# Preparing the first scan unit inside the routing program, and spreading the scatters over two units

## The reference

```
hidden [8,512,256]
layer 0, mixer : a two-directional state space layer (512 channels, 16 states):
                 xn = layernorm(x); xz = W_in xn; per direction: 4-tap convolution, silu,
                 x_dbl = Wx x -> dt (64), B (16), C (16); dt = softplus(Wdt dt + b)
                 for each state n: h[t] = exp(dt*A[n]) * h[t-1] + dt*B[n]*x ; y += C[n]*h
                 y = (y_forward + y_backward + x*D) * silu(z); s = W_out y
layer 0, experts: scores = Wr xn (8 experts), the best 2 of each token, weighted;
                 each expert: silu(a)*b of a 256->1024 product, then 512->256
layer 1        : linear attention with a memory (16 heads, chunks of 128), a three-level MLP
                 (256->1024->256) and a gate from W x + C V^T x
```

## Time and profile before

| | us |
|---|---|
| median of 3 runs (3166.04 to 3168.67) | 3166.66 |
| the profiled execution | 3172.15 |
| its span, first to last instruction | 3170.4 |
| TensorE / VectorE / ScalarE / GpSimd busy | 2612.1 / 2253.1 / 1776.4 / 1738.3 |
| granted TensorE clock, mean | 0.922 |

### The profile page before, as it was taken

One profiled execution on the slowest core, in us unless ns is written; L12 is line 12 of the kernel. 1 busy time (PEld: TensorE's weight loads), 2 busy tenths in 40 slices (PEclk: granted clock), 3 DMA queues, 4 the chain that ended last, 5 costly groups with the idle time before them and its releaser, 6 DMA issues. The chain is left out here.

```text
span 3170.4 us, 40091 instructions
## 1 busy us (share of the span) xinstructions
PE 2612.1 (82%) x13342; PEld 1723.8 (54%) x13342; DVE 2253.1 (71%) x2790; ACT 1776.4 (56%) x2731; POOL 1738.3 (55%) x550
## 2 busy tenths in 40 slices
PE   5357788787787887878878878657999999999999
PEld 5134565565565565565555555545556455555554
DVE  5399999989989989989989989984343442442430
ACT  1367777767867958858858858522332332332322
POOL 0598879869878878878778788851000000000000
PEclk9777899899999989989989989767999999999999
DMA  6223333333334333324333333213000000000000
GB/s 254 84 77 120 111 110 116 133 117 118 111 115 141 115 107 122 131 88 145 112 103 126 136 107 118 70 53 116 26 33 0 33 33 0 33 33 0 7 7 7
DMA packets 144229, 274.85 MB, mean 87 GB/s; under 512 B 23095, under 2 KB 94238, under 8 KB 143006
## 3 DMA queue, kind: packets, MB, share of 16 engines
q1 hardware_dynamic: 137886, 255.70, 23.7%
q0 software_dynamic: 6144, 16.79, 1.6%
HBM read 231.80 MB, written 40.63 MB: 86 GB/s over the span
## 5 line engine op out<-in xcount | busy, mean ns | idle before, releaser
L745 POOL TENSOR_TENSOR hs<-u,bb 128x2048 f32<-128x2048 f32 x256 | 1159.0, 4536 | 288.4 <-PE hT L1087 249.0
L947 DVE TENSOR_TENSOR_SCAN hs<-dA,hs 128x1024 f32<-128x1024 f32 x512 | 1163.1, 2278 | 96.5 <-POOL hs L745 72.6
L1087 PE MATMUL hT<-ident,hs 128*128 128x128 f32 x3616 | 586.3, 304 | 362.2 <-DVE held L957 312.1
L842 ACT ACTIVATE dA<-dt,cols 128x511 f32<-128x511 f32 x1024 | 661.4, 680 | 318.0 <-DVE hs L947 313.0
L1087 PEld LDWEIGHTS hT<-ident,hs 128*128 128x128 f32 x3616 | 443.5, 154 | 521.8 <-DVE held L957 370.5
L957 DVE SCALAR_TENSOR_TENSOR held<-hT,ct,held 128x512 f32<-128x512 f32 x872 | 604.5, 733 | 22.7 <-PE hT L1087 22.1
L1361 ACT ACTIVATE gl<-bank,cols_sb 128x512 f32<-128x512 f32 x192 | 130.7, 687 | 527.1 <-PE bank L1600 526.8
L1600 PE MATMUL bank<-mT,cms_sb 128*128 128x512 f32 x768 | 362.6, 597 | 10.1 <-ACT mT L1355 8.6
L138 POOL COPY cur<-slot 128x8 uint32 (+1 forms) x8 | 1.5, 190 | 626.7 <-DVE held L150 626.2
L1106 PEld LDWEIGHTS moe<-xgT,held 128*128 128x128 f32 x2272 | 289.0, 205 | 54.3 <-issue 26.4
L1106 PE MATMUL moe<-xgT,held 128*128 128x128 f32 x2272 | 302.9, 290 | 13.0 <-ACT xgT L857 13.0
(11 more groups left out here) (232 smaller groups left out, 3295.6 us busy)
## 6 DMA issues: line engine op xcount, KB each, us to landing
held<-wl SPq DMA_DIRECT2D x71, 1024.0 KB
bb<-b_scratch SPq DMA_DIRECT2D x128, 512.0 KB
held<-wl SPq DMA_DIRECT2D x71, 512.0 KB
xg<-xg_scratch SPq DMA_DIRECT2D x71, 128.0 KB
yg_scratch<-yg SPq DMA_DIRECT2D x71, 128.0 KB, 1.7
held<-x SPq DMA_DIRECT2D x16, 512.0 KB, 8.6
xg_scratch<-zero SPq DMA_DIRECT2D x8, 1024.0 KB, 4.7
cb<-b_scratch SPq DMA_DIRECT2D x30, 256.0 KB, 4.4
```

What stands on the lines that cost most here:

```text
L745: nc.gpsimd.tensor_tensor(hs[n % HS][:, :, :], u[d][:, :, :], row, ALU.mult).then_inc(dBu_ready, 1)
L842: last = nc.scalar.activation(dst, src, ACT.Exp, scale=cols[:, at:at + 1])
L947: nc.vector.tensor_tensor_scan(h, decay, h, 0.0, ALU.mult, ALU.add).then_inc(scan_done, 1)
L1087: last = nc.tensor.transpose(hT[c % 2][:, k * P:(k + 1) * P], hs[n % HS][:, k, c * P:(c + 1) * P], ident[:, :])
```

## The change

- **The first unit's preparation moves into the routing program.** Its products stand between the turns and scores of the batches on TensorE, its copies between the roots and copies on ScalarE; the weights are loaded between the batches of `x`. The eight products that build the convolution's `taps` move from VectorE to GpSimd; `xpad`'s second copies from VectorE to ScalarE. Batch 0 is turned straight into `xnT`, which is no longer stored and loaded. `soft` of the first unit is the end of VectorE's routing program. B's rows are stored and the first two pairs loaded there too.
- **Scores turned round**: `w_r`, widened to 32 columns, is stationary and `xaT` moves (two products of 512 columns a batch, four batches in one bank), then four transposes a half. Choice and weights are worked out in two halves of 16 chunks.
- VectorE takes the variance of batch b+1 before it normalises batch b, and ScalarE's roots stand one batch ahead.
- **Scatters over two units**: none before the first state; 8 chunks (`EARLY`, now 8) in states 0 to 2 of unit 0, one chunk in each of its other 13 states, 11 in unit 1. VectorE waits for the first eight before its first weighing, no longer before the unit loop.
- **Tiles**: unit 1 has one (at slot 25), units 2 to 15 five each. The first tiles are loaded at state 11 of unit 1.

```diff
-        EARLY = 18
+        EARLY = 8
+        OPEN = 3
+        GROUPED = 11
...
-                    last = scores(b)
+                def scores(b):
                     pe.wait_ge(aT_ready, KD * (b + 1))
+                    g, h = b % QB, b // QB
+                    for k in range(KD):
+                        last = nc.tensor.matmul(bankR[4 + h][RG * g:RG * (g + 1), :], w_r[:, k, :], xT(b)[:, k, :],
+                                                start=(k == 0), stop=(k == KD - 1))
...
+                turn_rows(0); turn_rows(1); scores(0); piece("proj", 0)      # TensorE, one line each in the code
+                turn_rows(2); scores(1); piece("proj", 1); turn_rows(3); scores(2)
+                piece("conv", 0); piece("proj", 2); turn_rows(4); scores(3); piece("conv", 1); piece("proj", 3)
+                turn_rows(5); turn_scores(0); scores(4); piece("conv", 2); turn_rows(6); scores(5)
+                piece("conv", 3); turn_rows(7); scores(6); scores(7); turn_scores(1)
+                piece("xd", 0); piece("dt", 0); piece("dt", 1)
+                pe.wait_ge(chosen, 2)      # the two counting products, then c, dt 2, dt 3
...
+                choose(0)                  # VectorE
+                choose(1)
+                weights(0)
                 dve.wait_ge(cnt_ps, 1)     # rows and owners as before
...
+                weights(1)
+                dve.wait_ge(setup_a, 1)
+                nc.vector.tensor_scalar(a_cols, a_cols, -1.0, None, ALU.mult)
+                for quarter in range(4):
+                    soft(dve, 0, 0, quarter)
...
-                for c in range(TC - EARLY, TC):
-                    group(c, grouped[0])
+                def groups(unit, n):
+                    if unit_is_first(unit):
+                        return range(TC - EARLY, TC)[3 * n:3 * n + 3] if n < OPEN else (n - OPEN,)
+                    return (NS - OPEN + n,) if unit_is_first(unit - 1) and NS - OPEN + n < TC - EARLY else ()
...
-                            if not later(unit) and n < TC - EARLY:
-                                group(n, grouped[1])
+                            for c in groups(unit, n):
+                                group(c, grouped[int(c < TC - EARLY)])
...
-                for i in range(-T0, 0) if d == 0 else range(NT - TPB * (NB - 1) if last else TPB - T0):
+                for i in range(1) if first else range(FIRST_TILE[d], FIRST_TILE[d] + TPU):
```

More of the change, by code:

```diff
@@ L20 @@
 HP = P // 2
+QB = NB // 2
+RG = P // QB
+QC = NC * QB
 EPS = 1e-5
@@ new lines, in plan @@
+        def plan(d, what, at):
+            for k, s in enumerate(at):
+                PREP[d][s].append((what, k))
+        plan(0, "proj", (0, 1, 4, 7))
+        plan(0, "conv", (3, 6, 8, 10))
+        plan(0, "silu", (10,))
+        plan(0, "xd", (12,))
+        plan(0, "dt", (14, 16, 18, 20))
+        plan(0, "soft", (21,))
+        plan(0, "c", (16,))
+        plan(1, "gate", (20, 21, 22, 24))
+        plan(1, "conv", (4, 6, 7, 8))
+        plan(1, "silu", (8,))
+        plan(1, "xd", (10,))
@@ new lines, in bass_mamba_moe_then_linear_attention_mlp @@
+        plan(1, "dt", (11, 12, 13, 15))
+        plan(1, "soft", (16,))
+        plan(1, "c", (17,))
+        OUT = {0: 0, 2: 1}
+        SKIP = (0, 2, 3, 4)
+        SOFT = ((13, 14, 15, 15), (15, 15, 15, 15))
+        LATE = ((3, 6, 15, 19, 21, 23, 28), (3, 5, 6, 16, 17, 18, 19, 20, 21, 22, 25, 28, 30))
+        FIN = (0, 0, 1, 1)
+        WEIGH, ADD = ((1, 2), (2, 2)), ((3, 3), (3, 3))
+        USES = [[use for s in range(2 * NS) for use in PREP[d][s] if use[0] not in ("silu", "soft")] for d in range(2)]
@@ L329, in tt, with variance @@
                     ch.link(nc.vector.tensor_tensor(o, a, c, op))
-                for b in range(NB):
+                def variance(b):
                     cs = range(NC * b, NC * (b + 1))
@@ L341, in _ @@
                     nc.vector.tensor_scalar(rs[:, cs[0]:cs[-1] + 1], mv[:, cs[0]:cs[-1] + 1, 1], EPS, None, ALU.add).then_inc(var0, 1)
+                variance(0)
+                for b in range(NB):
+                    cs = range(NC * b, NC * (b + 1))
+                    if b + 1 < NB:
+                        variance(b + 1)
                     dve.wait_ge(std0, b + 1)
@@ L359, in _ @@
[L359 to L370, removed]
+                def over(row, whole):
+                    return row.rearrange("p (c e) -> p c e", c=1).broadcast_to(whole)
@@ L408, in _ @@
[L408 to L412, removed]
+                weights(1)
+                dve.wait_ge(setup_a, 1)
+                a_cols = cols[:, AL:AL + 2 * DB * NS]
@@ L585, in units @@
                 for d in range(2):
-                    yield d, 2 * b + d, tile_pieces(d, last) if d == 1 or later(b) else NONE, not (last and d == 1)
+                    yield d, 2 * b + d, tile_pieces(d, not later(b)) if d == 1 or later(b) else NONE, not (last and d == 1)
             def batches(eng, body):
@@ L593, in batches @@
                 body(NB - 1, True)
-            def unit_is_first(unit):
-                return not later(unit)
             block = lay0.enter_context(nc.Block())
```

630 lines of the change are left out of this document (353 added, 277 removed).

## The result

The changed kernel takes 3161.41 us (median of 20 runs, 3155.33 to 3167.34) against 3166.87 us of the kernel before on the same chip (20 runs): ratio 0.9981, interval 0.9974 to 0.9988. So it is 0.2% faster there. On another chip, where the kernel before takes 3154.66 us, the same two kernels gave 1.0022 (1.0013 to 1.0031), 0.2% slower. The second comparison came with the experiments, and it is the more instructive one.

A forecast was written before the change was run, and what follows sets the result against it. It saw TensorE, then VectorE, leading the routing, an engine-to-engine preparation chain, and GpSimd and VectorE in units 0 and 1. Terms -57.2 + 29.4 + 3.1 + 15.8 = -8.9 us gave a median of 3158, range 3144 to 3173.

The forecast's parts named there:

- First state at 90.3, -57.2: Routing and preparation: unit 0's first state starts near 90.3 us instead of 147.54, -57.2 us, bounds -63 and -50.
- TensorE's 48.3 us of work: Routing: TensorE's turns, scores, projections, convolutions and score transposes until the second half's scores are turned, summed to 48.3 us.
- The GpSimd `taps`: Routing: eight operations, some 10 us on GpSimd, needed only near 30 us; no cost was added for them.
- The score product, bounds 1.0 and 3.58: Routing on TensorE: a batch's two products of 512 columns taken at a projection's 1.92 us; 3.58 was the old form.
- the three "remote" waits: Old preparation: ScalarE waits of 3.63, 8.06 and 3.67 us that no engine or transfer explains.
- The first rival: Routing: the 15.4 us of unexplained ScalarE waits move along with the preparation, giving 3173 us; chance 0.12.
- Scatters, +17.8 and +11.6: Units 0 and 1: scatters between states add 17.8 us in unit 0 and 11.6 in unit 1, +29.4 in all.
- the rival with 27.5: Unit 1: GpSimd's idle time doesn't take the scatters, costing up to 27.5 us instead of 11.6; chance 0.18.
- Last unit +3.1: Last unit: four more tiles, three of whose gates on VectorE fall before the last scan, +3.1 us, bounds 0 and 4.
- Tail +15.8: Tail: the gather waits for the store of the last tile's `down`, now at slot 30; +15.8 us, bounds 12 and 20.
- Everything behind shifts whole: After the tail's gather: the norm, the output and the barrier behind it shift whole, by the tail's +15.8 us.
- The rule weighed: Routing: crossing instruction blocks is mostly hidden and a taken branch stalls, so the long straight program costs nothing; time 3158.

The follow-up runs named there:

- e_taps: The changed kernel with the eight taps made by VectorE behind its normalisation of the third batch, not by GpSimd: 3161.88 us, ratio 1.0021 to the kernel before.
- e_oldscores: The changed kernel with the scores' products as before, 8 columns each and nothing turned: 3183.54 us, ratio 1.0089 to the kernel before.
- e_noscatter: The changed kernel with the 64 scatters and the waits for them left out: 3122.70 us, ratio 0.9897 to the kernel before.
- e_tail: The changed kernel with the last unit's five tiles five slots apart, starting at 0, 5, 10, 15, 20: 3151.81 us, ratio 0.9991 to the kernel before.

## Why the prediction was right, and where it was not

The forecast of 3158 us, range 3144 to 3173, has the time, 3161.4, in it. Its sum of -8.9 us stands against -4.9 in the profiles and -5.5 in the medians of that chip. Step by step:

- *First state at 90.3, -57.2*: 91.34, -56.2. Right as a sum, and by luck in its parts. The first turn came at 11.87 (forecast 11.3), the last scores at 64.2 (63; the forecast's own terms, 11.3 + 48.3 + 4.2, give 63.8). But TensorE's 48.3 us of work were counted at rows of both of its speeds, turns at 1.95 and products at 1.92, and the work took 43.2, as six of eight turns took 1.04 to 1.09. Its waits took 9.1 instead of 4.2: 5.10 for VectorE, 2.24 and 1.80 for the copies of scores. The two errors cancel. The GpSimd `taps`, put at nothing because they "are needed only near 30", are the term that failed: they blocked VectorE, for 3.7 us at the first state (`e_taps`).
- *The score product, bounds 1.0 and 3.58*: 1.90 was right, but 3.58 was no price of the old form. It was measured on a TensorE that waited 0.69 us ahead of every such group; without gaps it is 1.85 (`e_oldscores`). The granted clock is 1.00 in both stretches; the durations alone show the two speeds, and in these rows the slower one stands where TensorE has a gap in each batch.
- *What the change gains over the kernel before*: the three "remote" waits in the earlier trace rows were in the 57.2 as a gain. The first rival asked whether they would move along; none did. The question that was missing is whether the kernel before has them on every chip. On a chip without them the gain is 42.3, and the same change is slower. The forecast less these 14 us is +5 there. That the change came out faster hangs on the chip, and the prediction's reasons don't cover that: this too is luck.
- *Scatters, +17.8 and +11.6*: +17.8 and +11.0. That unit 1's idle time takes the scatters when GpSimd is last held, and the rival with 27.5 was wrong. `e_noscatter` gives the 38.2 us back when they are gone.
- *Last unit +3.1*: +2.3. *Tail +15.8*: +14.3, with ScalarE's copy at 2096.00, a wait of 10.10 us where about 11 were forecast; `e_tail` shows the cause.
- *Everything behind shifts whole*: within what an execution does. The head's 5.7 us more in the first pair weren't repeated.
- *The rule weighed* (no stall from the long straight program): the routing shows no "remote" wait. But the place of the program isn't free: where TensorE's loop comes to lie was worth 24 us in each of two kernels. The change happened to leave it well placed, which the prediction didn't ask.

## What to carry to other kernels

A wait that no engine and no transfer explains should be looked for in a second execution on another chip before a gain is counted on it; an edit that moves the work around it will be credited with it. Take the price of TensorE's work from rows of the speed at which it will run in its new place, and look for the same operation at both. After any edit that changes TensorE's program ahead of a loop, compare the loop's turns with its straight first pass, and the number of instruction blocks on the page with that of the kernel before: here twenty idle instructions were worth 22 us.

## What the hardware showed that was not expected

- GpSimd's products of two operands in SBUF blocked VectorE's scaling from SBUF to SBUF: four took 4.39 and 2.09 us instead of 1.38, and 1.38 again when GpSimd was idle, the same shape taking one product of GpSimd (1.1 us) for each of its own operations; the batch statistics at 18.78 beside it took their usual 1.39. The Trainium skill (SBUF — State Buffer, section SBUF: two separate sides) says that the two engines share a port as an exclusive lock, held for a whole instruction, which a two-port mode of VectorE also needs. The trace agrees that VectorE is held for a whole instruction of GpSimd. That this scaling runs in such a mode it doesn't show: alone it takes as long as the batch statistics of the same shape (1.38 and 1.39), which were not held.
- TensorE behind a loop's branch waits for a block of its instructions (1.1 to 2.1 us in the kernels before and after), and depending on where its program lies for a second one: 1.93 and then 2.58 us a few instructions later, or 3.99 to 4.73 at once. A turn is 3 to 6 us longer by it.
- The same program starts its first state at 147.54 us on one chip and at 133.45 on another. Why is not settled, nor why single executions differ by up to 7 us in units 2 to 14 (1600.1 to 1607.0 without the longer turns) and 8 in the head.
